# Two transformer layers on one core: GpSimd's roots ahead of its weight parts, the FFN mean on VectorE, and the rounded half of a rotated block on ScalarE

## The reference

```python
# layer 0: attention over segments of 2 tokens with 16 persistent keys, and a ternary linear layer
x = x + _L0_attn_ref(xn, ...) + _L0_ffn_ref(xn, ...)
# layer 1, attention: 32 query heads on 4 key heads of 64, rotary embedding, causal
qkv = jnp.einsum('bsh,oh->bso', hidden_states, w_qkv).reshape(b, s, HQ + 2 * HKV, D)
q, k = _rope(q, pos), _rope(k, pos)    # concat([x1*cos - x2*sin, x2*cos + x1*sin])
attn = jax.nn.softmax(jnp.where(causal, q @ k.T * D ** -0.5, min))
out = (attn @ v).reshape(b, s, HQ * D) @ w_o
# layer 1, FFN: ternary weights, layer norms inside
h = gelu(bitlinear(x, w_fc)); ffn = bitlinear(h, w_proj)     # bitlinear(x, w) = layer_norm(x) @ ternary(w).T
```

## Time and profile before

| | us |
|---|---|
| median of 3 runs (406.72 to 406.94) | 406.86 |
| profiled execution | 406.81 |
| its span, first to last instruction | 405.0 |
| TensorE busy (matmuls) | 369.5 (91%) |
| VectorE busy | 303.5 (75%) |
| ScalarE busy | 251.1 (62%) |
| GpSimd busy | 285.9 (71%) |

### The profile page before, as it was taken

The page is one execution under the profiler, slowest core; times in us unless marked ns, Lnnn a source line. Parts: engine busy times, 40 slices in busy tenths (PEclk is TensorE's granted clock), DMA queues, the critical chain, the costliest instruction groups (busy, mean ns, idle before and its releaser), DMA issues.

```text
span 405.0 us, 8415 instructions
## 1 busy us (share of the span) xinstructions
PE 369.5 (91%) x2852; PEld 347.6 (86%) x2868; DVE 303.5 (75%) x675; ACT 251.1 (62%) x808; POOL 285.9 (71%) x250
## 2 busy tenths in 40 slices
PE   3994686999999979699999999999999999999995
PEld 1664574999889979699999999999999999998985
DVE  4876596786787658467977887787778778787883
ACT  1346466347598465466776757677775758677671
POOL 3445337647999999999877987677798867777000
PEclk9998699899999989879999999999999999999999
DMA  8995010522333333534434563443447344433200
GB/s 262 413 408 217 1 32 21 130 55 68 79 89 94 81 77 81 135 84 95 116 79 104 137 161 91 100 104 91 100 113 180 88 98 95 110 85 78 79 2 26
DMA packets 34219, 45.15 MB, mean 111 GB/s; under 512 B 5505, under 2 KB 25986, under 8 KB 33794
## 3 DMA queue, kind: packets, MB, share of 16 engines
q1 hardware_dynamic: 34032, 44.62, 41.2%
q10 hardware_dynamic: 146, 0.00, 0.0%
HBM read 13.14 MB, written 1.05 MB: 35 GB/s over the span
## 4 chain that ended last, share of the span: by engine, by line
PE 66%; POOL 18%; DVE 6%; ACT 3%; issue 3%; DMA 3%; SPq 1%; POOLq 0%
PE bank L1266 14%; PE bank L1229 11%; PE bank L992 10%; PE bank L1286 10%; PE bank L1179 9%; PE bank L1138 3%; POOL woT_lo L607 2%; PE bank L1114 2%; POOL split_lo L660 2%; POOL split_hi L658 2%; POOL rope_b L650 2%; POOL rope_a L659 2%; POOL qkvT_lo L607 2%; PE bank L1232 2%; POOL rope_a L648 2%
## 5 line engine op out<-in xcount | busy, mean ns | idle before, releaser
L519 ACT ACTIVATE bank<-bank,neg_max 128x256 f32<-128x256 f32 (+1 forms) x256 | 101.3, 397 | 6.0 <-DVE neg_max L910 5.8
L528 ACT ACTIVATE probT_hi<-bank 128x512 fp32r<-128x512 f32 x96 | 57.6, 600 | 74.2 <-PE bank L992 74.1
L910 DVE TENSOR_REDUCE neg_max<-bank 128x2 f32<-128x512 f32 (+1 forms) x96 | 66.0, 688 | 38.2 <-PE bank L1232 26.7
L1266 PE MATMUL bank<-probT_hi,v 128*128 128x256 f32 x384 | 76.7, 296 | 3.1 <-DVE probT_lo L932 2.4
L1229 PE MATMUL bank<-kT,qT 128*128 128x256 f32 (+1 forms) x512 | 75.1, 280 | 3.2 <-DMA qT<-split_lo 3.2
L650 POOL TENSOR_TENSOR rope_b<-turned,cst 128x512 f32<-128x512 f32 x36 | 46.4, 1290 | 36.2 <-DMA turned<-raw 36.1
L1229 PEld LDWEIGHTS bank<-kT,qT 128*128 128x128 f32 x512 | 68.3, 196 | 3.4 <-DMA qT<-split_lo 3.4
L932 DVE TENSOR_TENSOR probT_lo<-bank,probT_hi 128x512 fp32r<-128x512 f32 x96 | 65.4, 681 | 5.3 <-ACT probT_hi L528 5.2
L926 DVE TENSOR_TENSOR prob<-bank,rsum 128x512 f32<-128x512 f32 x96 | 66.4, 691 | 3.3
L1266 PEld LDWEIGHTS bank<-probT_hi,v 128*128 128x128 f32 x384 | 58.8, 190 | 6.2 <-DVE probT_lo L932 3.8
L992 PE MATMUL bank<-cst,prob 128*128 128x128 f32 x384 | 58.6, 276 | 3.1 <-DVE prob L926 2.1
(11 more groups left out here) (155 smaller groups left out, 746.5 us busy)
## 6 DMA issues: line engine op xcount, KB each, us to landing
turned<-raw SPq DMA_DIRECT2D x144, 64.0 KB, 2.0
qT<-split_hi SPq DMA_DIRECT2D x64, 128.0 KB, 2.4
qT<-split_lo SPq DMA_DIRECT2D x64, 128.0 KB, 2.4
wq0T<-in_L_attn_w_qkv_dram SPq DMA_DIRECT2D x4, 512.0 KB, 8.2
wout<-in_L_attn_w_out_dram SPq DMA_DIRECT2D x4, 512.0 KB, 12.7
nat_qkv<-in_L_attn_w_qkv_dram SPq DMA_DIRECT2D x2, 1024.0 KB, 20.9
nat_o<-in_L_attn_w_o_dram SPq DMA_DIRECT2D x1, 2048.0 KB, 21.6
kT<-split_hi SPq DMA_DIRECT2D x16, 128.0 KB, 2.4
```

Of the source, the lines that this page charges most:

```text
L519: ins = nc.scalar.activation(own, own, ACT.Exp, bias=neg_max[it % 2][:, first + j:first + j + 1], accum_out=sums[it % 2][:, first + j:firs ...
L528: nc.scalar.activation(probT[0][:, n % 4, :], bank[2 + n % 2][:, :], ACT.Copy).then_inc(t_hi, 1)
L910: dve.tensor_reduce(neg_max[n // UNITS % 2][:, unit_columns(n % UNITS)], score_bank(n)[:, :].rearrange("p (h k) -> p h k", h=heads), AX.X, ...
L1266: ins = pe.matmul(group_bank(), v[b % 2][:, DH * z:DH * z + P], p, start=m == 0, stop=m == last)
```

## The change

1. GpSimd does the roots ahead of most weight parts: `weights_lo(0, 1)`, `batch_root(0)`, `weights_lo(1, 3)`, and so on; each `tile_root` stands ahead of the block sums that it stood behind or between. ScalarE copies weight unit 0 ahead of the signs and the absolute sum, and loads its gelu table earlier.
2. TensorE turns batch 0's tokens behind `ffn_0(3)` and `attention_0(3)`, and VectorE does `add0(2)` and `add0(3)` ahead of the scale and low half of batch 0.
3. `hidden_factors(t)` moves one step later, to just ahead of `ffn_add(t)`.
4. The mean part becomes one VectorE instruction per tile, in slots 6 to 13, in place of two on GpSimd.
5. For the 32 blocks from number 4 on, the hi half is a ScalarE copy of the full sum, made in the slot four behind the block's fill; GpSimd no longer makes it, and waits for it before lo. ScalarE writes one weight unit more per step in steps 0 to 6.

```diff
-        HI_IN = {0: 4, 1: 5, 2: 6, 3: 7, 4: 8, 5: 9, 6: 10, 7: 12}
+        HI_IN = {0: 5, 1: 6, 2: 7, 3: 8, 4: 9, 5: 10, 6: 11, 7: 12}
...
+            nc.scalar.activation(table_use[:, 0:1], table_use[:, 1:2], ACT.Gelu)
             act.wait_ge(p0_T, 1)
...
+            def high_rotated(n):
+
+                act.wait_ge(rope_done, summed(n))
+                if n >= 2:
+                    has_landed(act, n - 2)
+                nc.scalar.activation(split[0][:, n % 2, :, :], rope_a[:, n % 2, :].rearrange("p (j t) -> p j t", j=2),
+                                     ACT.Copy).then_inc(split_hi, 1)
+
             def slot(n):
                 if 2 <= n < N_UNITS + 2:
                     probs_T(n - 2)
+                for f in BLOCKS[OWN_HIGH:]:
+                    if FILL_SLOT[f] + 4 == n:
+                        high_rotated(BLOCK[f])
                 if n < N_UNITS:
                     probs(n)
...
-            weights_hi(0, 3)
+            weights_hi(0, 1)
+            sign(1, nat_fc[:, :, :], fcT[:, :, :], tern_fc)
...
+            weights_hi(1, 3)
...
-            weights_lo(0, 2)
+            weights_lo(0, 1)
             batch_root(0)
-            weights_lo(2, 3)
+            weights_lo(1, 3)
             batch_root(1)
...
-                pool.tensor_tensor(hi, a, z, ALU.add)
+                if n < OWN_HIGH:
+                    pool.tensor_tensor(hi, a, z, ALU.add)
                 own_done(pool.tensor_tensor(a, a, z, ALU.add))
+                if n >= OWN_HIGH:
+                    pool.wait_ge(split_hi, n - OWN_HIGH + 1)
                 pool.tensor_tensor(lo, a, hi.bitcast(F32), ALU.subtract).then_inc(split_done, 1)
...
-                weights_lo(2 * n + 1, min(2 * n + 3, len(W_UNITS)))
-                if n - 4 < TILES:
-                    mean_part(n - 4)
+                weights_lo(2 * n + 2, min(2 * n + 4, len(W_UNITS)))
...
+            def mean_part(t):
+
+                if t == 0:
+                    dve.wait_ge(wcol_done, 1)
+                dve.wait_ge(f_add, t + 1)
+                part = x[:, t // 2, t % 2, :]
+                dve.scalar_tensor_tensor(part, wcol[:, :], ffac[:, t, 4:5], part, ALU.mult, ALU.add).then_inc(f_mean, 1)
+
             def slot(n):
+                if 6 <= n < 6 + TILES:
+                    mean_part(n - 6)
...
-                    hidden_factors(t)
+                if t >= 1:
+                    hidden_factors(t - 1)
+                    ffn_add(t - 1)
...
-            turn_tokens(0)
             ffn_0(3)
             attention_0(3)
+            turn_tokens(0)
```

More of the change, by code:

```diff
@@ L162, in build @@
         wcol = at("wcol", 186 * K, [P, DIM])
-        mcol = at("mcol", 187 * K, [P, DIM])
         abs_out = at("abs_out", 164 * K, [P, FF // P * DIM])
@@ L180, in build @@
         lo0_done = sem("lo0_done")
-        tern_in, nb_done, ones_done, wcol_full, wcol_done, f_mean, mean_made = (
-            sem(n) for n in ("tern_in", "nb_done", "ones_done", "wcol_full", "wcol_done", "f_mean", "mean_made"))
+        tern_in, nb_done, ones_done, wcol_full, wcol_done, f_mean = (
+            sem(n) for n in ("tern_in", "nb_done", "ones_done", "wcol_full", "wcol_done", "f_mean"))
         zeroed, blk_zero, blk_done = sem("zeroed"), sem("blk_zero"), sem("blk_done")
@@ L194, in build @@
         v_zero = sem("v_zero")
-        raw_done, rope_done, split_done = sem("raw_done"), sem("rope_done"), sem("split_done")
+        raw_done, rope_done, split_done, split_hi = sem("raw_done"), sem("rope_done"), sem("split_done"), sem("split_hi")
         turn_landed = [sem(f"turn_landed{i}") for i in range(2)]
@@ L209, in build, with summed @@
         STEPS = TILES + 2
+        def summed(n):
+            return 2 * n + 2
         def of_batch(it):
@@ L236, in build @@
                 + [f for it in range(ITS) for u in range(UNITS) for f in fills_at(it, u)])
+        OWN_HIGH = sum(f[0] != "v" for fs in FILLS_IN.values() for f in fs)
+        FILL_SLOT = {f: UNITS * it + u for it in range(ITS) for u in range(UNITS) for f in fills_at(it, u)}
         PREPARED = sum(map(len, FILLS_IN.values()))
@@ L449, in _ @@
             nc.scalar.activation(m0[0:2 * H, :], bank[7][0:2 * H, 0:DIM], ACT.Copy).then_inc(m_done, 1)
-            sign(1, nat_fc[:, :, :], fcT[:, :, :], tern_fc)
-            act.wait_ge(ld["proj"], 16)
-            nc.scalar.activation(abs_out[:, :], nat_proj[:, :, :].rearrange("p c n -> p (c n)"), ACT.Abs,
-                                 accum_out=wsum[:, 2:3]).then_inc(proj_sum, 1)
             def weight_hi(n):
@@ L543, in slot @@
                     empty(fills_at(n // UNITS, n % UNITS))
-            nc.scalar.activation(table_use[:, 0:1], table_use[:, 1:2], ACT.Gelu)
-            weights_hi(0, 3)
+            weights_hi(0, 1)
+            sign(1, nat_fc[:, :, :], fcT[:, :, :], tern_fc)
+            act.wait_ge(ld["proj"], 16)
+            nc.scalar.activation(abs_out[:, :], nat_proj[:, :, :].rearrange("p c n -> p (c n)"), ACT.Abs,
+                                 accum_out=wsum[:, 2:3]).then_inc(proj_sum, 1)
+            weights_hi(1, 3)
             normal1(0)
@@ L664, in tile_root @@
                 root(ffac[:, t:t + 1, 1:2], t + B + 3)
-            def mean_part(t):
-                if t == 0:
-                    pool.wait_ge(wcol_done, 1)
-                pool.wait_ge(f_add, t + 1)
-                pool.tensor_tensor(mcol[:, :], wcol[:, :], ffac[:, t, 4:5].to_broadcast([P, DIM]), ALU.mult).then_inc(mean_made, 1)
-                pool.wait_ge(mean_made, t + 1)
-                part = x[:, t // 2, t % 2, :]
-                pool.tensor_tensor(part, part, mcol[:, :], ALU.add).then_inc(f_mean, 1)
-                pool.wait_ge(f_mean, t + 1)
+            weights_lo(3, 5)
             batch_root(3)
-            weights_lo(3, 4)
-            tile_root(0)
-            weights_lo(4, 5)
             pool.wait_ge(ld["rope"], 16)
             rope_products(0)
+            tile_root(0)
+            rope_sums(0)
             tile_root(1)
-            rope_sums(0)
+            weights_lo(5, 6)
+            rope_products(1)
             tile_root(2)
-            rope_products(1)
+            rope_sums(1)
             tile_root(3)
-            rope_sums(1)
+            weights_lo(6, 7)
+            rope_products(2)
             tile_root(4)
-            rope_products(2)
+            rope_sums(2)
             tile_root(5)
-            rope_sums(2)
-            weights_lo(5, 6)
+            weights_lo(7, 9)
             tile_root(6)
@@ L697, in _ @@
             rope_sums(3)
-            weights_lo(6, 9)
+            weights_lo(9, 10)
             for n in range(4, len(BLOCKS)):
@@ L857, in _ @@
             stats1(1)
+            add0(2)
+            add0(3)
             hidden_scale(0)
@@ L959, in slot @@
                     empty(fills_at(n // UNITS, n % UNITS))
-            add0(2)
             stats1(2)
             tokens_lo(1)
-            add0(3)
             stats1(3)
@@ L977, in _ @@
                     hidden_scale(step + 1)
-                if t >= 1:
-                    ffn_add(t - 1)
                 empty(FILLS_IN.get(step, ()))
```

## The result

| | before | after |
|---|---|---|
| median, us | 406.9 (4 runs, 406.72 to 408.85) | 413.12 (4 runs, 411.14 to 414.74) |
| profiled execution, its span | 406.81, 405.0 | 412.86, 411.0 |
| busy: TensorE, VectorE | 369.5, 303.5 | 372.4, 310.6 |
| busy: ScalarE, GpSimd | 251.1, 285.9 | 269.4, 235.8 |

The ratio is 1.0134 (95% interval 1.0095 to 1.0172): slower by over 1%, clear of the noise, and outside the predicted range of 401 to 411. In the later comparisons the kernel before had medians of 408.5 to 408.6 (57 runs), so its first four ran short; whether by chance or by another chip is not shown. Against the later medians the change costs 4.6 us.

The account below looks back on a forecast made before the run. TensorE bounds the kernel almost everywhere, with few, large stops. Terms -9.4 + 1 - 11.4 + 3.6 + 0.5 + 5.9 + 2.2 + 8 = +0.4, corrected to -0.4: 406.4 us from 406.86; range 401 to 411.

Parts of the forecast that it names:

- The front: Stretch ahead of the attention loop: earlier roots and turned order make it 9.4 us earlier, between 7.5 and 11.
- about 60.3, when its gelu is done: In the front: when the third tile's transposes come, in us, against 64.53 before.
- at 0.8 less: Correction for VectorE's stalls in the front, taken at their worst in the -9.4; turns the sum +0.4 into -0.4.
- the front doesn't deliver: Rival, 0.05: signs, normal1(3) or VectorE hold fc(2) back, 3 us of the 9.4 stay away; 409 us.
- signs of being wrong: No ScalarE wait on the sums, TensorE stops in slots 6 to 13, or first loop slot under 7 us earlier.
- The mean part: Slots 6 to 13: VectorE's eight instructions take about 1.0 us each, costing +1 us, from 0 to +7.8.
- GpSimd's load: In the attention loop: GpSimd's backlog goes, and with it the 11.4 us lost in slots 12 to 23; -11.4.
- the first key block: Batch 1's key block, slots 13 and 14: ScalarE's copy waits for GpSimd; 5.45 us stop plus clock fall, +8.
- Key blocks 2 and 3: Key blocks of batches 2 and 3: ScalarE's copies wait for GpSimd; two 2.96 us stops, +5.9, and clock, +2.2.
- clock falls at all three key blocks: Rival, 0.14: at slots 16, 40 and 64 each stop costs 2.8 us in clock; 410.1 us.
- Copies at u = 4: Loop slots with u = 4: ScalarE's copy delays TensorE's heads_out by 0.45 us in eight iterations, +3.6.
- small stalls: Rival, 0.22: the three key-block stops leave the clock high or shorten its fall, front at -10.5; 401.0 us.

Follow-up runs that it names:

- Window: Changed kernel; ScalarE copies blocks 4 to 10 only, behind exponentials and heads_hi; weight units 16, 17 behind block 8; hidden_scale(1) early; mean parts at slot ends: 392.25 us.
- The front alone: Kernel before with parts 1 to 3 and ScalarE's one weight unit more per step; GpSimd makes all halves and the mean part: 400.31 us.
- loop_alone: Kernel before, its front and weight order kept, with parts 4 and 5 of the change alone: 420.27 us.
- scale1_early: Changed kernel with VectorE's hidden_scale(1) ahead of the low half of batch 1: 409.39 us.
- after_fill: Changed kernel with TensorE multiplying zeros in the start's gaps (5 products, then 7): 411.13 us.
- window_front: Window with batch_root(1) and batch_root(2) ahead of weight units 1 and 2, and hidden_scale(0) and batch 0's low half ahead of add0(3): 392.56 us.
- warm: window_front with TensorE multiplying zeros before its first input (5 products) and while awaiting the second piece (3): 393.39 us.
- before_fill: Kernel before with TensorE multiplying zeros in the start's gaps (5 products, then 7): 407.5 us.

## Why the prediction was wrong

**The start (0 in the sum, +1.8).** With the same 32 products ahead of it, the copy of `gT` comes at 15.9 to 19.1 us in the 14 profiles without filled gaps, whatever the kernel. The products come 0.43 us apart at first and 0.21 later. The profile of the kernel before was one of the quick ones, and quick again from there to the first loop slot (0.84 and 1.52 us ahead of the other two with its front). Filling the gaps removed the difference in three profiles of three, so idle TensorE there has a part in it; the medians say that it isn't all of the chance. No step of the prediction was about this, so this part of the miss is bad luck; the error was to set a sum against a single execution and trust it to the microsecond.

**The front ("I take ... 9.4", -6.5).** This step failed. Of its parts, the roots, y1 and fc(0) came as predicted once the start is taken off: y1's transposes at 39.34 - 1.83 = 37.5, fc(0) at 43.41 - 1.83 = 41.6. The 3.69 us stop is gone too. What failed is the step from there to the third tile's transposes, put at "about 60.3, when its gelu is done", with VectorE's stalls "at 0.8 less": the second tile's transposes already waited 3.79 us for VectorE, and the third's came at 65.24 - 1.83 = 63.4. Moving weight units 3 and 4 ahead of `batch_root(3)` had laid them over `hidden_scale(1)`, which cost 2.3 us on TensorE's path, with a lower clock behind. With `hidden_scale(1)` early the start is 1.37 us late, and less this the third tile's transposes come at 60.3 and proj(1) at 63.1, both as predicted; the first slot has 2.5 us back and comes 9.1 earlier. Part of the 2.9 us that the -6.5 lacks can be the quick profile of before, whose two fellows stand 0.84 and 1.52 later. I had the row for this, and used it for the mean part only. The rival "the front doesn't deliver", named with VectorE as a cause and given 5%, is what happened. Two of the prediction's own signs of being wrong came with it: the first loop slot is less than 7 us earlier, and TensorE stops in slots 6 to 13.

**The mean part (+1).** Mechanism and size held: mean duration 0.91 us where I had 1.0, and 1.9 us lost with slot 4 where the sum has 1.5. TensorE's stops in slots 6 to 13 are how this loss looks, although the prediction also named them as a sign of being wrong. Three places in the loop made no difference by the profiles.

**GpSimd's load (-11.4) and the first key block (+8).** Together -3.4 predicted, -3.6 measured; the 5.23 us stop was predicted as 5.45. Two terms of opposite sign agree here in their sum, so that each needs a look of its own. Window takes slots 12 to 23 from 47.42 to 39.57 us, which shows 7.85 of the 11.4; two stops of 0.91 and 2.11 are left there. Without these it would take 36.55, an estimate, and against that the kernel before loses 10.9 us in these slots and the changed one, with 44.29, 7.7: close to the 11.4 and the 8. The front alone, where the stops stay, shows that the loss is not tied to the front.

**Key blocks 2 and 3 (+8.1).** 2.75 us stops for 2.96. The first lost 4.67 in all, with 0.72 as the clock of the next 6 us, the second 4.04 at full clock, so more than its stop. The same stops in other profiles show what the clock adds: at slot 40, 3.56 and 3.86 us were lost where the clock stayed at 1.00 (loop_alone, scale1_early; slots 38 to 47), and at slot 64, 4.68 where it was 0.72 (after_fill; slots 62 to 68). So the clock costs 0.6 to 1.1 us at each and the stop with what follows 3.6 to 4.0, where the sum had 1.1 and 2.96. The version in which GpSimd makes the key blocks' half shows the cause: the series of GpSimd's operations between two copies. The rival "clock falls at all three key blocks" had the third wrong in the profile of the changed kernel, by chance: in that of after_fill the clock falls at all three.

**Copies at u = 4 (+3.6).** Seven stops of 0.47 or 0.48 us and one of 0.27 at slot 90; the slots lose 3.8 in all. They vanish with the copy behind `heads_hi`.

The miss of 6.7 us is thus 1.8 of chance in the start, 2.9 in the front, where the held-up VectorE makes 2.5, 0.8 for the correction that nothing bore out (it takes the sum from +0.4 to -0.4, and so to 406.4), 1.0 in all terms of the loop together, and 0.3 between the profiled execution and the median. With the failed step mended the kernel measures 409.39, inside the range, but still above the 408.5 of the kernel before. In the rival of small stalls the 0.7 for a front at -10.5 should be 0.3, the front being at -10.2 with the correction: 401.4 for 401.0. The front's upper end, -7.5, was too narrow, since a known mechanism was left out of it.

## What to carry to other kernels

When a wait can't be removed, ask what stands behind the waiting instruction: the same 2 to 3 us wait of ScalarE for GpSimd cost 2.75 us ahead of the exponentials and 0.93 behind them. When an engine is relieved only while it is overloaded, relieve it only there: with copies for 7 blocks instead of 32 slots 12 to 23 took 7.85 us less than before, and none of the stops came later. And whenever GpSimd's work is moved, look at which small VectorE instructions with SBUF inputs it now lies over; before an order is changed, follow the DMA queue that serves it as well.

## What the runs showed of the hardware

- A VectorE instruction with one large SBUF input is held by GpSimd too: the 128x2048 TENSOR_SCALAR took 2.32 us in window_front, where it started 0.05 behind a GpSimd subtraction of 1.29, and 1.28 in the changed kernel, where it came first. In the latter case GpSimd's two subtractions, started 0.35 behind it, took 3.33 us instead of 2.48. The Trainium skill, "SBUF — State Buffer", section "Who interferes with whom", says that tensor_scalar can run in a mode that uses the shared ports, and that the first to issue blocks the other; both rows agree.
- TensorE's granted clock reads 1.00 in the first 10 us of the profiles, also where the products come at half their later pace. In the version warm, which had worked since 1.1 us, a stretch at the same 0.43 us pace is recorded at 0.50, that is 1.2 GHz; so is one from 12 to 15 us in the version with the mean parts at the end of their slots, without any filling. So a granted clock of 1.00 at the start of a trace does not show that TensorE is at 2.4 GHz; the spacing of equal products does.
- Clock falls behind a stop are not tied to its length: none behind 2.75 us in slot 64, 0.72 over 6 us behind 2.75 in slot 40. Nor are they the same from one profile to the next: behind the 2.94 us stop before the key projection the clock of the next 6 us is 1.00 in the profile of the kernel before, and 0.72 in those of before_fill and loop_alone, which have the same code there. The prediction took the first as a sign that such a stop leaves the clock alone.
